# First tile, loads apart, and the shared expert and gate in three float32r products: one change to an attention and mixture-of-experts layer on Trainium2

## The reference

```python
scores = einsum('bhsd,bhtd->bhst', q, k) / (d * d * h)
out = einsum('bhst,bhtd->bhsd', softmax(scores), v)
x = layernorm(x + out.reshape(b, s, d * h) @ WO)          # eps 1e-5
probs = softmax(x @ gate_W)                               # 8 experts, the best two kept, weights to sum 1
y = 0.5 * gelu(x @ shared_W + shared_b)
y += sum over e of combine[e] * (gelu(x @ W1[e] + b1[e]) @ W2[e] + b2[e])
return layernorm(x + layernorm(y) * gamma + beta)
```

## Time and profile before

| What | Value |
|---|---|
| median of 3 runs | 1798.11 us (1796.39 to 1798.91) |
| the profiled execution's own time | 1808.56 us |
| its span, first to last instruction | 1806.8 us |
| mean granted clock of PE in it | 0.984 |
| busy: PE, DVE, ACT, POOL | 96%, 76%, 57%, 22% |
| attention, tokens, experts in the span | 0 to 1145.3, 1145.7 to 1324, from there |

### The profile page before, as it was taken

The page is one execution under the profiler, slowest core; times in us unless marked ns, Lnnn a source line. Parts: engine busy times, 40 slices in busy tenths (PEclk is TensorE's granted clock), DMA queues, the critical chain, the costliest instruction groups (busy, mean ns, idle before and its releaser), DMA issues. The chain is left out here.

```text
span 1806.8 us, 31962 instructions
## 1 busy us (share of the span) xinstructions
PE 1728.9 (96%) x10963; PEld 1186.9 (66%) x10963; DVE 1370.6 (76%) x2196; ACT 1026.3 (57%) x1529; POOL 400.3 (22%) x442
## 2 busy tenths in 40 slices
PE   8999999999999999999999999899679999999977
PEld 6555555555555555555555555699579999999972
DVE  6888888888888888788888898677746666565647
ACT  6555565655656565555655555476545555455537
POOL 1000000000000000000000000016656676677654
PEclk9999999999999999999999999899889999999998
DMA  5011111111111111311111111465224343233335
GB/s 181 30 42 42 36 36 42 36 40 42 37 36 36 44 35 41 121 47 36 36 42 36 42 36 36 147 206 195 97 74 93 90 90 87 47 91 87 90 61 172
DMA packets 80198, 127.10 MB, mean 70 GB/s; under 512 B 12752, under 2 KB 46736, under 8 KB 77776
## 3 DMA queue, kind: packets, MB, share of 16 engines
q1 hardware_dynamic: 61808, 98.27, 16.2%
q0 software_dynamic: 18272, 27.31, 7.6%
HBM read 86.72 MB, written 38.83 MB: 69 GB/s over the span
## 5 line engine op out<-in xcount | busy, mean ns | idle before, releaser
L459 ACT ACTIVATE a_e<-banks 128x1024 f32<-128x1024 f32 x512 | 483.2, 1032 | 257.9 <-PE banks L356 257.9
L569 DVE TENSOR_TENSOR a_esum<-a_esum,a_e 128x1024 f32<-128x1024 f32 x384 | 470.7, 1226 | 94.3 <-ACT a_e L459 60.1
L370 PE MATMUL banks<-a_e,a_v 128*64 128x512 f32 x2048 | 467.4, 598 | 0.0
L370 PEld LDWEIGHTS banks<-a_e,a_v 128*64 128x64 f32 x2048 | 135.4, 136 | 265.9 <-issue 242.7
L63 POOL MEMSET ident<- 128x128 f32 x1 | 0.2, 204 | 1121.7 <-POOLq L112 1121.7
L356 PE MATMUL banks<-a_qh,a_kh 64*128 64x512 f32 x1024 | 220.6, 425 | 2.7 <-DVE a_ql L507 1.2
L356 PE MATMUL banks<-a_qh,a_kl 64*128 64x512 f32 x1024 | 202.6, 389 | 0.0
L356 PE MATMUL banks<-a_ql,a_kh 64*128 64x512 f32 x1024 | 202.3, 389 | 0.0
L1813 ACT ACTIVATE e_g<-banks,e_b1c 128x256 f32<-128x256 f32 x280 | 115.5, 471 | 150.3 <-PE banks L1761 146.9
L356 PEld LDWEIGHTS banks<-a_qh,a_kh 64*128 64x128 f32 x1024 | 96.0, 183 | 142.8 <-issue 93.1
L1774 PE MATMUL banks<-e_w2h,e_hh 128*128 128x256 f32 x560 | 161.3, 288 | 3.0 <-issue 1.3
(11 more groups left out here) (238 smaller groups left out, 3342.9 us busy)
## 6 DMA issues: line engine op xcount, KB each, us to landing
attn_out<-a_ot SPq DMA_DIRECT2D x64, 256.0 KB, 2.0
a_inv<-inv_rows SPq DMA_DIRECT2D x126, 128.0 KB, 2.8
a_w<-w_qkv SPq DMA_DIRECT2D x32, 256.0 KB, 3.1
raw<-attn_out SPq DMA_DIRECT2D x4, 2048.0 KB, 8.0
t_ot<-attn_out SPq DMA_DIRECT2D x4, 2048.0 KB, 8.7
raw<-w_up SPq DMA_DIRECT2D x8, 1024.0 KB
raw<-w_down SPq DMA_DIRECT2D x8, 1024.0 KB
raw<-x_t SPq DMA_DIRECT2D x8, 512.0 KB, 9.3
```

The costliest lines, as they stand in the source:

```text
L370: mm = pe.matmul(o_acc[h * DH:(h + 1) * DH, :], v[quad % 2][:, n, head], e[(slot * ST + n) % NE][:, h * BANK:(h + 1) * BANK], start=n == 0 ...
L459: act.activation(e[t % NE], ring[n % RING], ACT.Exp, scale=SCALE).then_inc(e_ok, 1)
L569: dve.tensor_tensor(acc[:, :], acc[:, :], e[(slot * ST + n) % NE], ALU.add).then_inc(add_ok, 1)
```

## The change

1. **The first tile begins in the attention.** `wo`, halved, and the halves of tiles 0 and 1 are made in slots 60 to 63 (`EARLY_WO`, `EARLY_OT`), on ACT after the slot's exponentials and on DVE after its additions and ahead of `inverses`; `project(0)` follows `sums` on PE. Their buffers lie over others of the attention that are no longer used. Tokens begins with `project(1)`, and its constants on DVE move from step 0 to step 4.
2. **Loads apart.** The loads of the attention's output and of x have semaphores of their own; the cast waits for the first alone, and the first is issued as soon as `ot_low` has freed its buffer, no longer after `add` too.
3. **Shared expert and gate in three float32r products.** `copy_turned` now casts to `t_x2th`; a new subtraction on DVE, `turned_low(n)`, makes `t_x2tl` out of PSUM; `branch(n)` waits for it and has six products in place of two of float32. `wgs` is split once (ACT in step 1, DVE in step 2).
4. **The opening.** Norms of rows and their maxima stand one unit later; POOL makes the identity first, and PE, ACT and DVE wait for its last instruction before their first use of the ones.
5. `rank`, `places` and `lows` of a part come one step later, and the experts' `w2h`, `w2l`, `hh` share places with the halves above.

```diff
+EARLY_WO = (SLOTS - 4, SLOTS - 3)
+EARLY_OT = (SLOTS - 2, SLOTS - 1)
...
@@ attention, PE, after the last slot @@
             sums(SLOTS - 1)
+            project(pe, keep, banks, 0)
...
@@ attention, DVE, at the end of a slot (ACT has wo_high and ot_high in the same slots) @@
+                if slot in EARLY_WO:
+                    wo_low(dve, keep, first["wo"], EARLY_WO.index(slot))
+                if slot in EARLY_OT:
+                    ot_low(dve, keep, first["ot"], EARLY_OT.index(slot))
                 if slot < SLOTS - 1:
                     inverses(slot)
...
@@ opening, PE @@
-                if 4 <= n < 4 + B * NB - 1:
-                    row_norms((n - 4) // NB, (n - 4) % NB)
+                if 5 <= n < 5 + B * NB - 2:
+                    row_norms((n - 5) // NB, (n - 5) % NB)
                 if n == 10:
+                    row_norms(B - 1, 0)
...
@@ tokens, SP @@
                 if h >= 2:
                     sp.wait_ge(otl_ok, (h - 1) * HALF)
+                load_ot(sp, keep, ot[h % 2], attn_out, h)
+                if h >= 2:
                     sp.wait_ge(r_done, (h - 1) * HALF)
-                load_half(sp, keep, ot[h % 2], xr[h % 2], attn_out, x_rows, h)
+                load_rows(sp, keep, xr[h % 2], x_rows, h)
...
@@ tokens, PE, branch(n) @@
                 for kk in range(KD):
-                    mm = pe.matmul(banks[4 + n % 2][:, 0:GS], x2t[n % 2][:, kk, :], wgs[:, kk, :], start=kk == 0,
-                                   stop=kk == KD - 1)
+                    for m, (lhs, rhs) in enumerate(((x2t_h, wgs_h), (x2t_l, wgs_h), (x2t_h, wgs_l))):
+                        mm = pe.matmul(banks[4 + n % 2][:, 0:GS], lhs[n % 2][:, kk, :], rhs[:, kk, :],
+                                       start=kk == 0 and m == 0, stop=kk == KD - 1 and m == 2)
...
@@ tokens, ACT, copy_turned(n) @@
-                act.copy(x2t[n % 2][:, :, :].rearrange("p a b -> p (a b)"), banks[2 + n % 2][:, 0:D]).then_inc(x2t_ok, 1)
+                act.copy(x2t_h[n % 2][:, :, :].rearrange("p a b -> p (a b)"), banks[2 + n % 2][:, 0:D]).then_inc(x2t_hi, 1)
...
@@ tokens, DVE @@
+            def turned_low(n):
+
+                lowered.add(n)
+                dve.wait_ge(x2t_hi, n + 1)
+                dve.tensor_tensor(x2t_l[n % 2][:, :, :].rearrange("p a b -> p (a b)"), banks[2 + n % 2][:, 0:D],
+                                  x2t_h[n % 2][:, :, :].rearrange("p a b -> p (a b)").bitcast(F32), ALU.subtract)\
+                   .then_inc(x2t_ok, 1)
...
                 if t + 2 < TT:
-                    ot_low(t + 2)
+                    ot_low(dve, keep, ot[(t + 2) // HALF % 2], t + 2)
+                if t == 2:
+                    dve.tensor_tensor(wgs_l[:, :, :], wgs, wgs_h[:, :, :].bitcast(F32), ALU.subtract)
+                for n in turned_after(t - 1) if t else ():
+                    if n not in lowered:
+                        turned_low(n)
```

More of the change, by code:

```diff
@@ L97, in load_ahead, with ot_high, ot_low, wo_high @@
     sp.dma_start(first["sbias"], shared_b.partition_broadcast(P)).then_inc(keep["c_in"], 16)
-    load_half(sp, keep, first["ot"], first["xr"], attn_out, x_rows, 0)
+    load_ot(sp, keep, first["ot"], attn_out, 0)
+    load_rows(sp, keep, first["xr"], x_rows, 0)
+def ot_high(act, keep, ot, t):
+    act.wait_ge(keep["ot_in"][t // HALF % 2], t // HALF // 2 * 16 + 16)
+    if t >= SPLITS:
+        act.wait_ge(keep["y_done"], t - SPLITS + 1)
+    act.copy(keep["oth"][t % SPLITS][:, :, :], ot[:, :, t % HALF * P:(t % HALF + 1) * P]).then_inc(keep["oth_ok"], 1)
+def ot_low(dve, keep, ot, t):
+    dve.wait_ge(keep["oth_ok"], t + 1)
+    dve.tensor_tensor(keep["otl"][t % SPLITS][:, :, :], ot[:, :, t % HALF * P:(t % HALF + 1) * P],
+                      keep["oth"][t % SPLITS][:, :, :].bitcast(F32), ALU.subtract).then_inc(keep["otl_ok"], 1)
+def wo_high(act, keep, wo, part):
+    these = slice(part * 4, part * 4 + 4)
+    act.wait_ge(keep["c_in"], 48)
+    act.copy(keep["woh"][:, these, :], wo[:, these, :]).then_inc(keep["woh_ok"], 1)
+def wo_low(dve, keep, wo, part):
+    these = slice(part * 4, part * 4 + 4)
+    dve.wait_ge(keep["woh_ok"], part + 1)
+    dve.tensor_tensor(keep["wol"][:, these, :], wo[:, these, :], keep["woh"][:, these, :].bitcast(F32), ALU.subtract)\
+       .then_inc(keep["wol_ok"], 1)
+def project(pe, keep, banks, t):
+    pe.wait_ge(keep["otl_ok"], t + 1)
+    u = t % SPLITS
+    oth, otl, woh, wol = keep["oth"][u], keep["otl"][u], keep["woh"], keep["wol"]
+    for a in range(PAIRS):
+        if t == 0 and a % 4 == 0:
+            pe.wait_ge(keep["wol_ok"], a // 4 + 1)
+        for m, (lhs, rhs) in enumerate(((oth, woh), (otl, woh), (oth, wol))):
+            mm = pe.matmul(banks[t % 2][:, 0:D], lhs[:, a, :], rhs[:, a, :], start=a == 0 and m == 0,
+                           stop=a == PAIRS - 1 and m == 2)
+    mm.then_inc(keep["y_done"], 1)
 def attention(nc, banks, keep, x_t, w_qkv, attn_out, raw, x_rows, w_o, w_gs, shared_b):
@@ L170, in attention @@
         ot_out = keep["ot_out"]
+        first = ahead(raw)
         Q, K, V = range(3)
@@ L716, in pe_general @@
                             mm.then_inc(g_pv_done, 1)
+            pe.wait_ge(g_e_done, B * PAIRS * UNITS + 1)
+            project(pe, keep, banks, 0)
         def act_general(act):
@@ L745, in act_general @@
                         act.copy(g_et, banks.both[1]).then_inc(g_et_evac, 1)
+            for part in range(2):
+                wo_high(act, keep, first["wo"], part)
+                ot_high(act, keep, first["ot"], part)
         def dve_general(dve):
@@ L771, in dve_general @@
                                             o_ps[h * DH:(h + 1) * DH, 0:P]).then_inc(g_o_evac, 1)
+            for part in range(2):
+                wo_low(dve, keep, first["wo"], part)
+                ot_low(dve, keep, first["ot"], part)
         block = ctx.enter_context(nc.Block())
@@ L859, in tokens @@
         ahead_of = ahead(raw)
-        wo, wgs, sbias = ahead_of["wo"], ahead_of["wgs"], ahead_of["sbias"]
+        wgs, sbias = ahead_of["wgs"], ahead_of["sbias"]
         ot = [ahead_of["ot"], sb("t_ot1", [P, PAIRS, HALF * P])]
         xr = [ahead_of["xr"], sb("t_xr1", [P, HALF, D])]
-        woh, wol = sb("t_woh", [P, PAIRS, D], R32), sb("t_wol", [P, PAIRS, D], R32)
-        oth = [sb(f"t_oth{u}", [P, PAIRS, P], R32) for u in range(SPLITS)]
-        otl = [sb(f"t_otl{u}", [P, PAIRS, P], R32) for u in range(SPLITS)]
+        for half in "hl":
+            keep["ot" + half].append(sb(f"t_ot{half}2", [P, PAIRS, P], R32))
         stats = sb("t_stats", [P, TT, 6])
@@ L1058, in _ @@
         def _(pe):
-            def project(t):
-                pe.wait_ge(otl_ok, t + 1)
-                if t >= 2:
-                    pe.wait_ge(r_done, t - 1)
-                u = t % SPLITS
-                for a in range(PAIRS):
-                    if t == 0 and a % 4 == 0:
-                        pe.wait_ge(wol_ok, a // 4 + 1)
-                    for m, (lhs, rhs) in enumerate(((oth, woh), (otl, woh), (oth, wol))):
-                        mm = pe.matmul(banks[t % 2][:, 0:D], lhs[u][:, a, :], rhs[:, a, :], start=a == 0 and m == 0,
-                                       stop=a == PAIRS - 1 and m == 2)
-                mm.then_inc(y_done, 1)
             def turn(n):
```

126 lines of the change are left out of this document (64 added, 62 removed).

## The result

| | us | ratio to before |
|---|---|---|
| kernel before, median (5 runs) | 1798.11 (1794.75 to 1799.03) | |
| kernel after, median (5 runs) | 1835.49 (1835.40 to 1837.44) | 1.0219, 95% 1.0208 to 1.0230 |
| after, profiled execution | 1835.75, span 1834.0 | |
| before, profiled execution | 1808.56, span 1806.8 | |

Slower, as forecast, but by 37.4 us where the sum said 25.4. The forecast of 1823.5 missed by 12 us, and 1835.49 lies just above the range of 1808 to 1835. The stages of the changed kernel, as windows of its trace (columns of the earlier trace rows): the start of tokens to branch(0), the 23 steps to branch(23), the last tiles with ranking and sort, and the experts' stage, which here means from the first turn of gathered rows to the end.

What follows compares the result with a forecast made beforehand. PE was taken as the bound in the steps of tokens (busy 93.99 of 95.32 us). Terms -1.2 - 3.4 + 23.0 + 2 + 5 gave +25.4, so 1823.5 us from the median 1798.11; range 1808 to 1835.

Steps and rivals of the forecast that it cites:

- Opening, -1.2: In the opening, norms one unit later fill most of PE's 2.26 us idle time: -1.2 us, bounds 0 and -1.4.
- project(0) and the front, -3.4: Between attention and branch(0), project(0) runs in DVE's reciprocal and branch(0) comes at about 1168.8: -3.4 us, bounds -7 and 0.
- Clock at 1.00 from 1146 on: Sign of being right: PE at full clock from the start of tokens at about 1146.
- The branch, 0.74: In each step of tokens, six products of 264 columns take 0.74 us against 0.89.
- The ring, +23.0 and +2: In tokens' 23 steps, the new subtraction closes a ring through PE, ACT, DVE: +23.0 us; `top` and `places` on DVE: +2.
- rival B: In tokens' steps, PE's clock also falls to half in nearly every group: +36 us, 1859; 3 in 100.
- Rival A: In tokens' steps, the ring isn't closed and PE remains the bound: -10.7 us, 1787.4; 8 in 100.
- C: In tokens' steps, only the two long steps of each group are held, ordinary ones 4.0: +11 us, 1809; 5 in 100.
- Last tiles, +5: After branch(23), four steps with two subtractions each before their branches and one more ring step: +5 us, bounds 0 and +8.
- What follows keeps its work: After the last tiles, ranking, sort and experts keep their work and are only shifted, clock low before as after.
- The median is 10.45 lower: The whole kernel's forecast is given from the median 1798.11, 10.45 us under the profiled execution's 1808.56: 1823.5 instead of 1834.0.
- Rival D: Whole kernel: the change does only its first part, the opening's -1.2 us, and 0 elsewhere: 1797; 1 in 100.

Runs made afterwards that it cites:

- before_again: The kernel before, unchanged, profiled once more: 1796.37 us.
- low_first: The changed kernel with the turned rows' subtraction moved ahead of ot_low on DVE in every step: 1812.45 us (1.0082).
- plain_together: The changed kernel with the old float32 branch, loads together again, e_hh at its old place and e_xh, e_xl, e_g in the lower part: 1794.82 us (0.9987).
- fill: The changed kernel with unused products on PE ahead of the waits of branch(2) to branch(23): 1836.01 us (1.0214).
- low_twice: The changed kernel with a second subtraction of the turned rows on DVE ahead of the real one, tiles 0 to 22: 1847.77 us (1.0286).
- places_alone: The kernel before, every instruction in its order, with only the changed kernel's places in memory: 1804.19 us (1.0035).
- all_high: plain_together with e_xh, e_xl and e_g in the upper memory beside e_hh, and e_y, e_b2w and the weights below: 1785.60 us (0.9946).
- plain_branch: The changed kernel with only the split of the branch taken out, so the old float32 products: 1797.68 us (1.0004).

## Why the prediction was right in kind and short in size

From before_again (span 1794.6) to the changed kernel (1834.0) are 39.4 us, and the stages give them all: branch(0) 5.15 earlier, steps +31.15, last tiles to experts +6.51, experts' stage +6.89. The sum had -4.6 (opening and front), +25, +5 and 0. So it was 14 us short between these two profiles (12 between the medians), and two of its steps carry most of that: the experts' stage, taken at nothing, 6.9 us, and the ring, 6.2 us. Against the sum's own steps:

- **Opening, -1.2: held in place.** The hole is 0.89 us where it was 2.26, and 1.66 in before_again. The attention's last sums started at 1139.27, against 1139.75 and 1140.21, but they moved between 1137.7 and 1142.9 over all runs, so its worth isn't settled. Slots 62 and 63 delayed nothing that PE waited for.
- **project(0) and the front, -3.4: inside its bounds, with two errors against each other.** project(0) ran at 1140.23, beside the reciprocal. branch(0) came at 1167.86, forecast 1168.8. But the terms that the prediction names add up to 12.3 us, so that from 1157.6 they give 1169.8; 1168.8 comes out only when they are counted from 1156.5. They took 10.5 us (1157.38 to 1167.86). The load of the second half was what came next, PE idle 1.70 us for a forecast of 2.9; over the runs this stretch was 1.7 to 5.6 us. Over all runs the load took 8.0 to 10.9 us to land. What sets that isn't shown: with the third half issued 4.3 us after it, it took 8.6 us in the changed kernel and 10.9 in low_first, and without, 9.8 in plain_together.
- **"Clock at 1.00 from 1146 on": wrong.** It was at half from 1146.7 to 1150.0, behind 1.96 us of idle time, after which I had expected none.
- **The branch, 0.74: 0.84 measured.** Between products it is 0.12 as taken, but from the first one behind a wait to the second it is 0.22 (1190.00, 1190.22). Where the branch does not wait, as in 13 of 24 in low_first, it takes 0.74 us. The estimate from the Trainium skill's four passes for true FP32 (FP8 and Floating Point Precision, TensorE Precision Notes), 0.67, is farther off; the row was the better guide.
- **The ring, +23.0 and +2: right in mechanism, short by 6.** With the clock at 1.00 the 23 steps are 124.2 us (fill, 1167.55 to 1291.78) where the sum had 120.3. The steps shown are 4.53 and 6.05 us for 4.42 and 5.93; the branch's 0.10 explains nearly all of that, 2.3 us in 23 steps. Most of the rest is one step: from branch(1) to branch(2) it took 7.46 us, because the first gelu loads a table of its own on ACT ahead of the deviation's, which the sum did not have:

```profile
1173.72 1.28 ACT L1255 ACT_TABLE_LOAD   x1
1175.01 0.42 ACT L1255 ACTIVATE t_shared<-t_pre 128x256 f32<-128x256 f32 x1
1175.45 1.28 ACT L1234 ACT_TABLE_LOAD   x1
```

  The step behind the long one took 5.94 to 6.17 in fill for 5.81, an ordinary one with `top` 4.73. The last 2.3 us (126.5 less 124.2) are rival B's mechanism at a small price, half clock in five stretches of 3.4 us.
- **Order, not load: shown.** The Trainium skill (PSUM — Partial Sum Buffer, Engine vs sequencer instructions) calls VectorE's queue strict FIFO; low_first agrees, where the same subtraction one place earlier brought the 23 steps from 126.49 to 98.39 us. low_twice shows that the steps hang on the ring. Rival A, the ring not closed, and C, ordinary steps at 4.0, fell with the 4.53. PE's idle time before L1155 was 35.7 us where I had 20 to 30. Its share in the steps was 81% where I had 75: at half clock the same work counts as busy for twice as long.
- **Last tiles, +5: 6.5.** I had four subtractions ahead of their branches. I had missed that each pair is chained, branch(n), bias, t_x2tl(n+1), branch(n+1).
- **"What follows keeps its work": the step that failed most, +6.9 for 0.** The work is the same, 3568 products, but tensors of the stage lie elsewhere, and PE is busy for 449.5 us with it instead of 442.3. places_alone shows it without any other change. I had read the new places in the diff and costed them at nothing without a row.
- **"The median is 10.45 lower": held, and the agreement without it is chance.** The first profile of before was held up for 15 us in the experts' stage, so it was right to give the forecast from the median; before_again and the changed kernel both lie within 2 us of their medians. Profile to profile (1806.8 to 1834.0, +27.2) the sum looks good to 1.8 us, but only because some 12 us of hold-up in before's first profile hide the 14 that the sum lacks.
- **The change's gains, without its loss.** Opening and early tile, with the old branch, loads together and other places, give all_high, 10.7 us under the kernel before. Against before_again its branch(0) is 6.4 us earlier and its 23 steps take 92.87 us for 95.34; the stage, 468.3 for 467.6, is no part of the gain. The 2.5 us in the steps the prediction did not have, and which part of the change gives them wasn't tried. Rival D, only the first part working, had 1.2 in all.

## What to carry to other kernels

Before an instruction goes behind a waiting one on an in-order engine, follow what it releases in the same step: here one subtraction of 0.4 us, one place too late, cost 28 of 126 us in the steps, and the idle third of each engine said nothing of it. Cost a move in memory like any other change, and check it by the count of products in a stretch, since busy share and clock don't show it. Take a second profile of the kernel before when the first lies more than the spread of the runs from their median.

## What the runs showed of the hardware

- **A product's time depends on where tensors lie in SBUF, and not on its own operands' places alone.** Products of 256 columns in the experts' stage, all at clock 1.00, came 0.1134, 0.1178 or 0.1200 us apart, a level mostly kept through half a chunk (48 products) or more. Whole chunks (96 products and four turns), as the starts of the turns in before_again, once fast and once slow, and in places_alone:

```profile
1348.79 0.60 PE L1748 MATMUL banks<-ident,xg 128*128 128x128 f32 x4
1360.13 0.60 PE L1748 MATMUL banks<-ident,xg 128*128 128x128 f32 x4
...
1395.44 0.60 PE L1748 MATMUL banks<-ident,xg 128*128 128x128 f32 x4
1407.19 0.38 PE L1748 MATMUL banks<-ident,xg 128*128 128x128 f32 x2
```

```profile
1349.60 0.60 PE L1755 MATMUL banks<-ident,xg 128*128 128x128 f32 x4
1361.36 0.60 PE L1755 MATMUL banks<-ident,xg 128*128 128x128 f32 x4
```

  11.34, 11.75 and 11.76 us. The kernel before has both kinds, places_alone and the changed kernel only the slow one. Up products were at 0.1200 in all four kernels with e_xh in the lower part, and fast chunks were found only where e_xh and e_hh (for down: e_hh) lie above. The place of a product's own operands doesn't settle it: plain_branch and all_high have e_xh, e_xl and the up weights at the same addresses, and yet all up chunks are at 0.1179 in the one and 14 of 35 at 0.1134 in the other, where e_hh, e_hl, e_y and e_b2w moved. What in the addresses sets the level, and why it switches between chunks, stays open: it wasn't tried tensor by tensor.
- **Idle stretches of 2 us can be followed by half clock.** The idle time of 1.96 us at the border is the same in the twelve kernels with the early tile, and the clock fell behind it in five of them; behind 2.26 us in the opening it did not the earlier trace rows. In the steps of the changed kernel it fell five times, each 0.02 to 1.3 us after the end of a wait of 1.85 to 3.4 us; behind three waits of 1.97 to 2.07 us it did not, and behind the twelve waits of 0.35 to 1.22 us never. With PE filled it never fell there.
- **An early load can hold up a store.** With the loads apart (plain_branch), the store of t_shared issued at 1233.90, 2.6 us behind a load of 2 MB, took 7.8 us to land and kept gelu waiting 3.51 us to 1241.81. With the loads together (plain_together) the same store, with no new load beside it, landed after 3.5 us, the wait is gone and the 23 steps were 2.5 us shorter; other stores of that kernel took 8 us beside a load, but nothing waited for them. I had priced that part of the change at nothing, and in the changed kernel itself no gelu waited for a store.
